# The recurrent stage's opening for batch 0 moved into the cosine stage, the last slot's feed-forward into the recurrent steps

## The reference

```python
# cosine attention, 16 heads, per batch; its output is normalised, then added
x = x + layernorm(softmax(cos(q, k)) @ v @ Wout) * g_out
# feed-forward, per batch
y = (layernorm(x) @ W) * scale
y = y * tanh(|y|) / (|y| + eps);  y = y * min(0.99 / |y|, 1)
x = x + y
# recurrent (gated linear) attention, 16 heads, 8 key and 16 value channels each
q, k, v = xn @ Wq, xn @ Wk, xn @ Wv;  decay = exp(logsigmoid(xn @ Wgk1 @ Wgk2 + b) / 16)
S_t = decay_t * S_(t-1) + k_t v_t;  o_t = q_t S_t;  x = x + (rmsnorm(o) * silu(xn @ Wg)) @ Wo
```

## Time and profile before

| | |
|---|---|
| runs, median | 2189.97 us |
| profiled execution | 2190.11 us, its span 2188.4 us |
| mean granted TensorE clock | 0.969 |
| TensorE, VectorE, ScalarE, GpSimd busy | 1965.3, 1023.3, 812.9, 515.5 us |
| first block | 0 to 575 us |
| cosine block | 580 to 1424 us |
| recurrent block | 1427 to 1618 us |
| last block | 1620 to 2188 us |

### The profile page before, as it was taken

How to read it: one execution, slowest core, us unless ns; L and a number is a source line. 1 busy time by engine, 2 the same in 40 slices (tenths; PEclk the granted TensorE clock), 3 DMA queues, 4 the chain that set the end, 5 groups by cost and what they waited for, 6 DMA issues and landing times. The chain is left out here.

```text
span 2188.4 us, 30020 instructions
## 1 busy us (share of the span) xinstructions
PE 1965.3 (90%) x11522; PEld 1251.4 (57%) x11522; DVE 1023.3 (47%) x2231; ACT 812.9 (37%) x1786; POOL 515.5 (24%) x617
## 2 busy tenths in 40 slices
PE   6999999999899999999999999669857899999885
PEld 4556666566566766676677667523235554545653
DVE  4555555545223233333243322259955565556444
ACT  2554535545234233323332333135413234445332
POOL 2332322323001011111111010026631143542221
PEclk9999999999999999999999999879979999999998
DMA  5000000000200000000000000020000000000001
GB/s 224 1 1 1 1 1 1 1 1 1 74 1 1 1 1 1 1 1 1 1 1 1 1 1 1 1 69 0 0 1 1 1 1 1 1 1 2 1 1 39
DMA packets 9773, 24.01 MB, mean 11 GB/s; under 512 B 2449, under 2 KB 6305, under 8 KB 8865
## 3 DMA queue, kind: packets, MB, share of 16 engines
q1 hardware_dynamic: 8336, 18.92, 2.4%
q10 hardware_dynamic: 1296, 3.18, 0.4%
HBM read 20.00 MB, written 2.10 MB: 10 GB/s over the span
## 5 line engine op out<-in xcount | busy, mean ns | idle before, releaser
L1429 PEld LDWEIGHTS cos_ps<-cos_vx,cos_probs 128*128 128x128 f32 x2048 | 238.8, 191 | 33.6 <-issue 28.7
L1429 PE MATMUL cos_ps<-cos_vx,cos_probs 128*128 128x129 f32 x2048 | 239.8, 275 | 4.2 <-DVE cos_on L1158 4.2
L1420 PE MATMUL cos_ps<-lead_room,cos_kT 128*128 128x512 f32 x512 | 232.0, 598 | 7.4 <-PEq L50 6.1
L1322 ACT ACTIVATE cos_probs<-cos_ps 128x512 f32<-128x512 f32 x256 | 150.9, 598 | 186.7 <-PE cos_ps L1420 185.9
L671 ACT ACTIVATE probs<-sc,nmax 128x512 f32<-128x512 f32 (+3 forms) x256 | 132.3, 524 | 168.8 <-DVE nmax L525 166.7
L1244 POOL TENSOR_TENSOR cos_qrs<-cos_qse,neg_half 128x4 f32<-128x4 f32 x59 | 59.4, 1006 | 511.9 <-DVE cos_qse L1140 511.9
L780 PE MATMUL sc<-kT,qT 128*128 128x512 f32 (+3 forms) x512 | 172.2, 458 | 3.9 <-DVE probsT L537 2.6
L1420 PEld LDWEIGHTS cos_ps<-lead_room,cos_kT 128*128 128x128 f32 x512 | 94.8, 192 | 104.2 <-issue 101.5
L2743 DVE TENSOR_REDUCE cos_wq<-tail_ps 128x2 f32<-128x1024 f32 (+3 forms) x128 | 101.8, 823 | 82.4 <-PE tail_ps L2983 81.3
L1138 DVE TENSOR_REDUCE cos_qss<-cos_qsq 128x4 f32<-128x512 f32 x59 | 40.5, 686 | 194.4 <-ACT cos_qsq L1301 194.4
L752 PE MATMUL pq<-xnT,wap 128*128 128x512 f32 x256 | 124.9, 611 | 3.5 <-DVE swp L517 3.5
(11 more groups left out here) (431 smaller groups left out, 3444.6 us busy)
## 6 DMA issues: line engine op xcount, KB each, us to landing
onT<-in_mla_wqT SPq DMA_DIRECT2D x1, 2048.0 KB, 9.8
lead_room<-in_mla_wo SPq DMA_DIRECT2D x1, 2048.0 KB, 20.1
cos_wq<-in_cos_wq SPq DMA_DIRECT2D x1, 2048.0 KB, 25.7
cos_wout<-in_cos_wout SPq DMA_DIRECT2D x1, 2048.0 KB, 7.4
out<-x SPq DMA_DIRECT2D x4, 512.0 KB, 2.9
x<-in_x SPq DMA_DIRECT2D x1, 1536.0 KB, 15.3
wq_pe<-in_mla_wq_pe ACTq DMA_DIRECT2D x1, 1024.0 KB, 14.8
x<-in_x SPq DMA_DIRECT2D x1, 512.0 KB, 4.2
```

Source lines behind the costliest of these rows:

```text
L1322: act.activation(probs[:, n % 2, kj, :], ps[:, kj, :], ACT.Exp).then_inc(s["e_done"], 1)
L1420: pe.matmul(ps[:, kj, :], kT[:, b % 2, kj * P:(kj + 1) * P], qT[:, hq % 2, h % 4, :], start=True, stop=True).then_inc(s["s_ready"], 1)
L1429: last = pe.matmul(po[:, qi // 2, qi % 2, :], probs[:, n % 2, kj, qi * P:(qi + 1) * P], vx[:, b % 2, kj, :], start=(kj == 0), stop=(kj == ...
```

## The change

Six edits belong together.

1. In batch 3 of the cosine stage, heads 2 to 5 and 10 to 13 get pieces: turned rows, z1, q, z, k and v of the recurrent stage's batch 0. VectorE makes the row statistics in head 0 and the normalised rows in head 1, GpSimd the power between them, VectorE the gate's elementwise part (heads 10 and 12), ScalarE the exponential, logarithm and decay (heads 11 and 13). Results go to memory that both stages share (`g["gla"]`).
2. The "g" feed-forward of batch 3 is taken off the cosine stage's end. The cosine stage has six semaphores more (36).
3. The recurrent stage starts with `repeat(0)` and the two gate products; its waits for batch 0's opening are dropped, since the block before has done it.
4. The feed-forward of batch 3 goes into the recurrent steps: statistics in step (0, 2), rows in (0, 3), turned rows on TensorE in (0, 5) and (0, 6), products and their scaling in (1, 0) and (1, 1), squares in (1, 2), power and tanh in (1, 3), the finish on VectorE in (1, 5). Six semaphores more (26).
5. `yn` of the cosine stage shares memory with `fy`.
6. The last stages take their adapters, turned rows, queries and keys from memory of the recurrent stage instead of their own.

```diff
@@ cos_misc
+    if b + 1 == B:
+        pieces += {2: [("gla_rows", "r", 0, 0)], 3: [("gla_rows", "r", 0, 1)], 4: [("gla_z1", "r", 0, 0)],
+                   5: [("gla_q", "r", 0, 0)], 10: [("gla_z", "r", 0, 0)], 11: [("gla_k", "r", 0, 0)],
+                   12: [("gla_v", "r", 0, 0)], 13: [("gla_v", "r", 0, 1)]}.get(h, [])
@@ cosine_attention, vector
+                    if (kind, b) == ("g", B - 2):
+                        dve.wait_ge(s["p_ready"], filled["gla_rows", "r", 0, 1])
...
+                    if kind == "gla_z":
+                        dve.tensor_scalar(z, src, g["gla_bgk2"][:, 0:1], None, ALU.add).then_inc(s["by_v"], 1)
+                        dve.drain()
+                        dve.scalar_tensor_tensor(za[:, :], z, -1.0, z, ALU.mult, ALU.min).then_inc(s["za_ready"], 1)
...
+                        if b + 1 == B:
+                            if h == 0:
+                                layer_norm_stats(dve, rstats, rmv, rve[:, :], [x[:, i, :] for i in range(TI)], LN_EPS,
+                                                 s["rec_var"])
+                            elif h == 1:
+                                recurrent_rows()
+                            elif h == 12:
+                                dve.wait_ge(s["ln_ready"], 1)
+                                dve.scalar_tensor_tensor(z, z, 0.0, za[:, :], ALU.min,
+                                                         ALU.subtract).then_inc(s["lg_ready"], 1)
...
-                row_stats(B - 1)
-                norm_rows("g", B - 1)
-                for key in cos_ffn("g", B - 1):
-                    empty(key)
-                finish_ffn("g", B - 1)
@@ cosine_attention, scalar
+                        if b + 1 == B:
+                            if h == 11:
+                                act.wait_ge(s["za_ready"], 1)
+                                act.activation(za[:, :], za[:, :], ACT.Exp)
+                                act.drain()
+                                act.activation(za[:, :], za[:, :], ACT.Ln, bias=1.0).then_inc(s["ln_ready"], 1)
+                            elif h == 13:
+                                act.wait_ge(s["lg_ready"], 1)
+                                act.activation(rec["decay"][:, 0, :], z, ACT.Exp, scale=1.0 / GATE_NORMALIZER)
@@ gla_pieces
+    slots = {(0, 5): (("ffn_rows", B - 1, 0),), (0, 6): (("ffn_rows", B - 1, 1),), (1, 0): (("ffn_prod", B - 1, 0),),
+             (1, 1): (("ffn_prod", B - 1, 1),)}
@@ gated_linear_attention, vector
-                row_stats(0)
-                dve.wait_ge(g["late_loaded"], 16 * count)
...
+                    if (b, p) == (0, 2):
+                        ffn_stats()
+                    elif (b, p) == (0, 3):
+                        ffn_norm()
+                    elif (b, p) in ((1, 0), (1, 1)):
+                        ffn_scale(p)
+                    elif (b, p) == (1, 5):
+                        finish_ffn()
@@ gated_linear_attention, gpsimd
+                    if (b, p) == (0, 2):
+                        pool.wait_ge(s["ffn_var"], 1)
+                        pool.tensor_tensor(frstd, fve, g["neg_half"][:, 0:TI], ALU.pow).then_inc(s["ffn_rstd"], 1)
+                    elif (b, p) == (1, 3):
+                        pool.wait_ge(s["n2_ready"], 1)
+                        pool.tensor_tensor(norm, n2, g["pos_half"][:, 0:TI], ALU.pow).then_inc(s["norm_ready"], 1)
@@ gated_linear_attention, scalar
-                act.wait_ge(g["late_loaded"], 16 * count)
                 act.wait_ge(s["setup"], 1)
-                for p in range(GLA_PAIRS):
-                    project(0, p)
                 for t in range(GLA_STEPS):
                     b, p = divmod(t, GLA_PAIRS)
+                    if (b, p) == (1, 2):
+                        act.wait_ge(s["emptied_v"], emptied["ffn_prod", B - 1, 1])
+                        for i in range(TI):
+                            act.drain()
+                            last = act.activation(fsq, fy[:, i, :], ACT.Square, accum_out=n2[:, i:i + 1])
+                        last.then_inc(s["n2_ready"], 1)
+                        act.drain()
+                    elif (b, p) == (1, 3):
+                        act.wait_ge(s["norm_ready"], 1)
+                        act.activation(tf[:, 1, :], norm, ACT.Tanh).then_inc(s["tanh_ready"], 1)
@@ gated_linear_attention, tensor
-                pe.wait_ge(g["late_loaded"], 16 * count)
+                repeat(0)
                 for key in GLA_OPENING:
                     fill(key)
-                repeat(0)
```

## The result

The changed kernel takes 2178.79 us (median of four runs, 2175.47 to 2181.61) against 2190.25 for the kernel before beside it: ratio 0.9941, 95% interval 0.9928 to 0.9954, so about 0.6% faster where 0.87% was forecast. Its profiled execution took 2181.61 us (span 2179.9), 8.5 less than the profiled execution of before, where the sum said 19.1.

What follows compares the result with a forecast made beforehand. TensorE was taken to bound the last cosine batch, VectorE the recurrent steps, and no work the seam. Seam 42.2 less 13.0, 9.1, 0.4 and 0.6 gave 19.1 us off 2190.11: 2171.0 us, range 2165 to 2179.

Steps and rivals of the forecast that it cites:

- The bound now: TensorE sets the pace in the last cosine batch, VectorE in the recurrent steps; the seam between is engine-to-engine chains.
- part 1: Seam from the attention add to the first recurrent multiplication: 48.0 us becomes 5.8, so 42.2 us go.
- Part 2: Last cosine batch: eight added TensorE pieces cost 13.0 us more; ScalarE's table loads stay covered.
- Part 3: Recurrent steps: added VectorE work and new waits, less two vanishing waits, make 9.1 us more.
- the waits ahead of the scalings: Recurrent steps: VectorE waits for TensorE's two feed-forward products, ffn_prod 0 and 1, by 1.5 and 1.3 us.
- Steps 0 to 8: First recurrent steps: statistics 2.1, row scaling 1.45, 0.2 beside GpSimd, less a vanished wait of 0.91; 2.8 us more.
- the port pair: Recurrent steps: VectorE's row scaling and finish slowed beside GpSimd's multiplications, 0.2 each, 0.4 us in all.
- the failed step: Recurrent steps: VectorE's waits for the spreading, 0.91 and 1.34 us, vanish since TensorE doesn't fall behind a slower VectorE.
- Rival A: Recurrent steps: TensorE's clock stays low through the first batch, costing 27 us, time 2198; chance 4%.
- rival B: Recurrent steps: VectorE and GpSimd exclude each other for whole instructions, 2.5 us instead of 0.4, time 2174.5; chance 12%.
- Rival C: Added work blocks TensorE's queue in steps (1, 2) to (1, 4), or bank 7 waits; 2179, chance 8%.
- The semaphores: Ends of cosine and recurrent stages: six more to clear in each, 0.1 us a semaphore, 0.6 us per stage.

Runs made afterwards that it cites:

- e8: e3's kernel with both feed-forward product scalings, and the squares, power and tanh behind them, one step later; single execution 2161.77 us.
- e3: Changed kernel with the feed-forward's finish on VectorE moved from step (1, 5) to (1, 7), behind batch 0's second output add; 2172.05 us, ratio 0.9915.
- e5: Changed kernel with idle matmuls filling TensorE's waits: 20 ahead of batch 0's second output product, 10 ahead of batch 3's turned rows; single execution 2171.43 us.
- e7: Changed kernel with 30 unused semaphores more in the cosine stage; single execution 2175.25 us.
- e6: e3's kernel with row scaling (step (0, 4)) and finish (step (1, 7)) between VectorE's multiplications and scan; single execution 2171.15 us.
- e9: e8's kernel with e6's placement of row scaling and finish between VectorE's multiplications and scan; 2167.15 us, ratio 0.9896.
- e1: Changed kernel with only the opening moved into the last cosine batch, the feed-forward back at the cosine stage's end; 2184.97 us, ratio 0.9966.
- e10: The kernel of e8 again, unchanged, timed over four runs; 2165.92 us, ratio 0.988.
- e4: The changed kernel once more, unedited, for further runs and a second profile; 2176.26 us, ratio 0.9927.

## Why the prediction was right and wrong

**The bound now and part 1: right.** The seam gave 42.54 against 42.2. The lower clock at the first spreading was there (2.08), the gate products took 4.90 us and held nobody.

**Part 2: right.** 13.43 against 13.0, all of it on the forecast heads; ScalarE's two table loads (1.28 each) were covered, heads 12 to 14 being 8.72 to 8.73 apart where lateness would have shown.

**Part 3, the waits ahead of the scalings: right in place and size** (1.49 and 1.06 against 1.5 and 1.3), and e8 takes them away.

**Steps 0 to 8: right in the sum (3.07 against 2.8), in part by luck.** The step with the row scaling grew by 2.39 us instead of 1.65, while the first step came 0.30 shorter. With the finish moved (e3) the steps 0 to 24 grow by 9.2, and 2.0 of that is the port pair, for which the sum had 0.4; so, as an estimate, its other terms there were about 1.9 too high, which the sum alone doesn't show.

**Part 3, the failed step** is this one: "What is given back: VectorE's waits for the spreading, 0.91 at 1477.91 and 1.34 at 1524.56, vanish, since TensorE doesn't fall behind a slower VectorE." The first did vanish. For the second I had counted VectorE's own queue behind each added instruction and ScalarE's effect on TensorE, but not who waits for what VectorE does after it: the add that empties the first output product's bank stands behind the finish, the second product needs that bank, and TensorE takes its work in order. A VectorE delay of 4.6 us became a TensorE delay of 4.30, and TensorE came out of it with a low clock (3.78 instead of 1.99). VectorE then waited 2.90 where the sum had no wait at all. Both orders were there to be read in the code; I followed only one of them.

**Steps 16 to 24, missing from the sum, +3.0.** TensorE's wait for ScalarE's rows stood there before as well (1.79 us, transposes 1.06 us). In the changed kernel it is 2.13 us, and the clock falls behind it; e5 gives back 2.9 by filling it, e7 has the same 2.13 at full clock and 38.73 us, and in e3 a low clock there costs nothing, since VectorE has no wait for TensorE. Rival A named the low clock, and the sign given for it, a spreading of 2 us beyond the third step, did come (2.08 at 1527.70), but not a whole batch at half speed; what happened is two short stretches, 5.4 us together by e5, which no rival priced.

**The port pair: a term mis-sized.** 0.4 taken, 2.0 measured (e6). The bound was in rival B, whose rule from the Trainium skill (SBUF — State Buffer, SBUF: two separate sides), an exclusive lock for a whole instruction, the numbers bear out better than the row I took: four scalings of 1.39 took 2.46, and an instruction of 0.16 took 0.89 (1493.90 to 1494.79) and ended with GpSimd's multiplication (1494.77). A row of one long instruction says little about several short ones with drains between them; that each of these may be caught anew fits the 0.42 and the 0.89 in one finish, but was not tried by itself.

**Rival C's time, 2179, came out, by another way, which is luck.** It had the in-order queue of TensorE in it, but behind ScalarE in steps 10 to 12, and there nothing grew: TensorE waited 1.05 us for ScalarE's rows at 1478.72, under the 2.04 of before. In the cosine stage the lone products cost 1.72 each, as priced, so no bank wait came with them.

**The semaphores: mis-sized**, 0.07 us each for 0.1, 0.3 us too much in all. At the recurrent stage's end another 1.5 us were low clock at the last output products, whose addition waited 1.98 us at 1608.22 against 1.03; in e3 the stage's end took 26.93, which is before's 26.45 and the six semaphores.

**Outside:** +1.6 in the blocks ahead and +0.6 behind are of the size by which the same stretches differ between kernels that don't touch them (first block's end 572.97 to 578.30, last block 561.6 to 575.2).

## What to carry to other kernels

When work is put into the stream of an engine, follow not only what stands behind it on that engine but each buffer which that engine frees later, and ask which in-order engine wants it next; put it behind the last such release, as one moved call did here for 8.7 us over the stage's stretches. Price a wait of TensorE not by its length alone but by what it computes right after, since a gap of 1.5 to 4 us was followed here, though not each time, by matmuls at nearly half speed. Small VectorE instructions go where GpSimd is idle (2.0 us here), but that place is to pass the first rule too: in e6 and e9 it stood ahead of an add that frees a bank, and TensorE waited 1.79 and 1.43 us for it. A product gets a full step between the engine that makes it and the one that waits for it.

## What the runs showed of the hardware

- A gap doesn't set the clock alone. After waits of 2.03 and 2.04 us the same transposes took 1.94 and 1.06 us (e1, before), after 2.13 us in two kernels 1.94 and 1.06 (changed kernel, e7). After a gap of 2.19 us at the same place of the third batch (ahead of the spreadings at 1514.92 in e10, 1520.44 in e3) e10 kept full clock, while in e3 the sum behind the spreading took 1.92 us instead of 1.05; e9 lost the clock after 1.48 us of waiting. In the recurrent stage it came the same in both profiles of one kernel (changed and e4, e8 and e10), in the last block it did not; across small shifts of the work ahead it doesn't follow the gap. What decides is open.
- The last block, untouched by any of these edits apart from the memory it uses, takes one of several lengths (561.6 to 562.0, 567.3 to 568.6, 575.2 us over 13 profiles), in one pair of runs with a granted clock of 0.66 against 1.00 over 20 us. A single execution can't tell 6 us of this kernel; the stretches of the edited stage can, to 0.15 us.
- Clearing a semaphore at a block's end takes 0.071 us (30 more: 3.49 to 5.62 us, e7).
- An exponential, then a logarithm, then a tanh and exponentials on ScalarE took a table load of 1.28 us each way (1346.34 and 1348.28 in the changed kernel), with the next operation within 0.01 us of its end (1347.63 and 1349.57); in head 11 of the cosine batch neither delayed a head.
- Small VectorE instructions that met a GpSimd multiplication ended with it, 0.16 us alone becoming 0.89 and 0.17 becoming 1.06 (changed kernel, e3), but not all did: the reciprocal at 1493.64 took its 0.18 beside the same multiplication. The product scalings, which read PSUM, showed no growth (0.69).
